# Graph layer on one core: edge sums taken in turned form, without carry products, and crossing runs in one more tile

## Chip, core and metric

One NeuronCore of a Trainium2 chip runs the whole program. The metric is the device time in microseconds. Before the change it is 1387.75 us in the median of three runs (1385.13 to 1388.79).

## What is computed

Per node a row of 256 floats; 50,000 nodes and 12,500 edges. The targets `dst` are drawn unevenly (low numbers more often), the sources `src` evenly.

```python
def L0(x):                       # attention over the edges that end in a node
    h = x @ Wn.T + bn
    e = edge_attr @ We.T + be
    a = leaky_relu(sum((h[src] + e) * attn, -1), 0.01)
    a = exp(a - segment_max(a, dst)[dst])
    a = a / (segment_sum(a, dst)[dst] + 1e-16)
    return relu(segment_sum(h[src] * a[:, None], dst))
def L1(x):                       # mean over the rows of dst, summed by src
    mean = segment_sum(x[dst], src) / maximum(segment_sum(1, src), 1)[:, None]
    return x @ W1.T + b1 + mean @ W2.T + b2
x = layernorm(x + L0(x))
x = layernorm(x + L1(x))
```

## The kernel before, in words

The edges lie in T = 100 tiles of 128, four of them a group (GT = 4), so Q = 25 groups. The nodes lie in G = 98 groups of 512. Five stages follow each other.

1. **Sort.** The edges are ordered by target, then by source, by counting with one-hot products (`sort`, `tiles`, `starts`). `ordered_rows`, `ordered_columns` and `ordered_ends` (L896 to L923) turn the ordered keys into columns and into indices: `idx_src` and `idx_dst` for gathers, `idx_out` for scatters. `idx_out` holds the node in the last edge of a run of equal keys of a tile and a spare row or a number out of bounds elsewhere. For targets this runs inside the second sort; POOL then gathers the 100 tiles of `x[src]` into `X`. For sources it is hung into the node pass by `hooks` at groups HOOK = 48, 50 and 52.
2. **Logits and softmax** on VectorE (L1087 to L1141), with the row ends turned by PE. `weight` is the exponential of each edge, not yet divided.
3. **Target pass** (`by_dst`). `select` (L1024) makes per tile a matrix `sel` that is the edge's weight where row and column have the same key, and `csel` that marks which edges continue the run of the tile before. `aggregate` (L1324) takes `sel` times the tile's rows of `X`, plus `csel` times the summed rows of the tile before; so each tile waits for the ACT copy (`raw`, L681) of the one ahead of it. Column 256 of `X` is one, and its sum is the denominator. `scale` (L1045) divides, `turn_sums` (L1340) turns the rows by PE, ACT copies them to `xT`, `products` (L1279) multiplies by `wnT` on top of a bias product, ACT cuts at zero into `xin`, and POOL adds the rows into `z_dram` (L532), a copy of x. SP waits for all these adds before it loads the first nodes.
4. **Node pass** (`dense`). SP loads 512 nodes, VectorE takes statistics and normalises, PE turns (L1276) and multiplies by `w1T` (L1287), ACT scales, SP stores into `out`. Meanwhile POOL orders the sources and gathers `z[dst]` into `X`.
5. **Source pass** (`by_src`). The neighbours' sums are made as in stage 3, with `csel`, 258 columns (standard deviation and mean of each neighbour ride along) and `scale`. POOL gathers each edge's own node from `z_dram` (L484), VectorE normalises it, PE turns it, and `products` adds the terms with `w2T` and `w1T`. VectorE takes statistics, ACT writes `yout`, POOL scatters the rows over `out` (L487). DVE's turn q holds the own rows of group q and the result of group q - 2.

The engines run their lists in order. Around the change POOL's list sets the order:

```python
for q in range(Q + 3):
    ...
    if q >= 3:
        h = q - 3
        pool.wait_ge(s_ey, GT * h + GT)
        if q < Q:
            pool.wait_ge(s_xs[q % 4], 16 * GT * (q // 4 + 1))
        for j in range(GT):
            scatter(out, yout[h % 4][:, j, :], column(idx_out[SRC], GT * h + j), s_ysc[h % 4])
```

## Time and profile before

| | |
|---|---|
| median of 3 runs | 1387.75 us |
| profiled execution, its own time | 1386.75 us |
| its span in the trace | 1384.9 us |
| mean granted TensorE clock | 0.951 |
| PE, DVE, ACT, POOL busy | 86%, 77%, 52%, 54% |
| target pass, first to last scatter-add issued | 382 to 584 us |
| node pass, first load to last product | 588 to 1023 us |
| source pass | 1024 us to the end |

POOL is busy while it makes an indirect DMA; the transfer itself lands later. "issue" in the chain or behind an idle time means that the profile shows nothing that was waited for.

### The profile page before, as it was taken

To read this page: it belongs to the slowest core of one execution; us is meant where nothing else is said; L and a number is where in the kernel's file an instruction comes from. 1 tells how busy PE (TensorE), PEld (TensorE's weight loads), DVE (VectorE), ACT (ScalarE), POOL (GpSimd) and SP (SyncE) were. 2 spreads that over 40 slices of the span, in tenths; PEclk is the share of its full clock that TensorE was granted. 3 is DMA by queue.
4 is the path that set the end of the run, shared out by engine and by line. 5 is a ranking of instruction groups with operands and counts; after the bars stand their busy time and mean duration, and the time that the engine had idled before them with its cause. 6 is when DMAs were issued, how large, how long until landed. Compare 5 with 4: busy or idle time off the path is not lost.

```text
span 1384.9 us, 25745 instructions
## 1 busy us (share of the span) xinstructions
PE 1195.2 (86%) x6722; PEld 1032.0 (75%) x6722; DVE 1072.2 (77%) x4008; ACT 721.6 (52%) x1720; POOL 753.4 (54%) x731
## 2 busy tenths in 40 slices
PE   4778868970499999689999999999989998889994
PEld 3667758860388888478888888888868887778783
DVE  8799978889655555189999999999988876776761
ACT  4755764540144444357777767777754553434441
POOL 1077754777677777734444005565443565555663
PEclk9999999995699999889999999999999999999997
DMA  5999695878166666557777769999951322222221
GB/s 158 318 266 265 166 248 180 264 230 327 43 92 93 100 96 87 65 201 244 243 243 243 251 236 306 324 324 322 327 181 64 100 90 86 83 87 88 90 75 44
DMA packets 118436, 251.04 MB, mean 181 GB/s; under 512 B 23731, under 2 KB 63548, under 8 KB 118360
## 3 DMA queue, kind: packets, MB, share of 16 engines
q1 hardware_dynamic: 75738, 183.99, 41.7%
q0 software_dynamic: 40128, 64.45, 20.4%
q10 hardware_dynamic: 2494, 1.76, 0.4%
q8 instruction: 27, 0.44, 0.1%
q14 instruction: 49, 0.40, 0.1%
HBM read 172.65 MB, written 130.41 MB: 219 GB/s over the span
## 4 chain that ended last, share of the span: by engine, by line
PE 50%; DMA 12%; POOL 11%; DVE 11%; issue 9%; ACT 5%; SPq 1%; POOLq 0%; ACTq 0%; DVEq 0%
PE bank L1287 30%; PE bank L1276 8%; DMA xin<-z_scratch,idx_src 5%; POOL out_rows L487 5%; POOL xin L484 5%; PE bank L1337 4%; PE bank L1333 3%; PE bank L1264 3%; DMA X<-in_x,idx_src 2%; DVE X L769 2%; ACT aggn L624 2%; DVE bank L772 2%; DMA yout<-low_digits_scratch 2%; DVE xT L772 2%; DVE stats L936 2%
## 5 line engine op out<-in xcount | busy, mean ns | idle before, releaser
L1287 PE MATMUL bank<-w1T,xT 128*128 128x256 f32 x1968 | 459.2, 380 | 0.3 <-ACT yout L586 0.3
L1287 PEld LDWEIGHTS bank<-w1T,xT 128*128 128x128 f32 x1968 | 365.5, 190 | 48.4 <-issue 0.9
L493 POOL DMA_INDIRECT order_scratch<-pay,rank_i x200 | 194.7, 973 | 200.1 <-DVE xin L769 89.9
L936 DVE BATCH_NORM_STATS2 stats<-xin 128x6 f32<-128x512 f32 x246 | 158.7, 687 | 88.5 <-DMA xin<-z_scratch,idx_src 67.0
L577 ACT COPY xT<-bank 128x512 f32<-128x512 f32 x346 | 203.3, 589 | 19.8 <-PE bank L1276 11.7
L586 ACT ACTIVATE yout<-bank,rstd 128x256 f32<-128x256 f32 x492 | 207.3, 489 | 5.2 <-DVE rstd L1177 4.8
L685 ACT COPY agg<-bank 128x257 f32<-128x257 f32 (+1 forms) x200 | 74.3, 372 | 225.0 <-PE bank L1337 218.4
L532 POOL DMA_INDIRECT z_scratch<-xin,idx_out x100 | 156.4, 1564 | 53.2 <-ACT xin L698 30.0
L936 DVE BATCH_NORM_STATS2 stats<-bank 128x6 f32<-128x512 f32 x246 | 165.6, 682 | 22.8 <-PE bank L1287 22.7
L487 POOL DMA_INDIRECT out_rows<-yout,idx_out x100 | 100.0, 1000 | 139.3 <-DMA xin<-z_scratch,idx_src 73.5
L581 ACT ACTIVATE std<-stats,eps_c 128x4 f32<-128x4 f32 x271 | 81.0, 300 | 178.8 <-DVE stats L936 176.6
L769 DVE TENSOR_SCALAR xin<-xin,low_mean,rstd 128x256 f32<-128x256 f32 x492 | 170.7, 410 | 1.0
L484 POOL DMA_INDIRECT X<-z_scratch,idx_dst x100 | 96.0, 960 | 126.6 <-DVE xin L769 91.8
L1264 PE MATMUL bank<-sel,agg 128*128 128x196 f32 x800 | 156.8, 340 | 3.5 <-DVE bank L772 3.5
L1276 PE MATMUL bank<-ident,xin 128*128 128x128 f32 x984 | 133.4, 275 | 19.8 <-DVE xin L769 19.7
L1337 PE MATMUL bank<-agg,csel 128*128 128x257 f32 (+1 forms) x396 | 123.7, 394 | 24.9 <-ACT agg L685 24.9
L1276 PEld LDWEIGHTS bank<-ident,xin 128*128 128x128 f32 x984 | 117.9, 143 | 35.8 <-issue 20.2
L1264 PEld LDWEIGHTS bank<-sel,agg 128*128 128x128 f32 x800 | 133.5, 195 | 4.9 <-DVE bank L772 4.5
L1215 PE MATMUL bank<-X 128*128 128x196 bf16 x800 | 95.8, 256 | 36.4 <-ACT sel L672 21.2
L1333 PE MATMUL bank<-X,sel 128*128 (+2 forms) x400 | 122.7, 390 | 3.4 <-DVE csel L769 3.4
L484 POOL DMA_INDIRECT X<-in_x,idx_src x100 | 99.8, 998 | 45.4 <-issue 19.5
L484 POOL DMA_INDIRECT xin<-z_scratch,idx_src x100 | 99.6, 996 | 42.1 <-issue 30.5
(201 smaller groups left out, 1747.9 us busy)
## 6 DMA issues: line engine op xcount, KB each, us to landing
z_scratch<-in_x SPq DMA_DIRECT2D x125, 400.0 KB
xin<-z_scratch SPq DMA_DIRECT2D x97, 512.0 KB, 5.1
out_rows<-yout SPq DMA_DIRECT2D x97, 512.0 KB, 3.3
kB<-sorted_scratch SPq DMA_DIRECT2D x50, 256.0 KB, 3.4
yout<-keys_scratch SPq DMA_DIRECT2D x50, 128.0 KB
xin<-in_edge_attr SPq DMA_DIRECT2D x12, 512.0 KB, 9.9
yout<-low_digits_scratch SPq DMA_DIRECT2D x50, 64.0 KB
order_scratch<-pay,rank_i POOLq DMA_INDIRECT x200
```

What stands on the lines that cost most here:

```text
L484: g.indirect_dma_start(out=dst_ap, out_offset=None, in_=table, in_offset=where).then_inc(s, 16)
L487: g.indirect_dma_start(out=table, out_offset=where, in_=src_ap, in_offset=None, bounds_check=N - 1, oob_is_err=False).then_inc(s, 16)
L493: g.indirect_dma_start(out=order_dram[k], out_offset=bass.IndirectOffsetOnAxis(ap=rank_i[k][:, t:t + 1], axis=0), in_=pay[:, t, :], in_off ...
L577: a.copy(xT[dst_i][:].rearrange("p a b c -> p (a b c)"), src_bank[:, :]).then_inc(copied, 1)
L586: a.activation(yout[hu][0:rows, j, :], bank_of(j // 2)[0:rows, (j % 2) * D:(j % 2 + 1) * D], ACT.Copy, scale=rstd[0:rows, slot, j:j + 1]). ...
L769: return v.tensor_scalar(o, i, s1, s2, o0, o1) if o1 is not None else v.tensor_scalar(o, i, s1, s2, o0)
L936: return v.bn_stats(stats[0:rows, slot, 2 * p:2 * p + 2, :].rearrange("p j s -> p (j s)"), pair.rearrange("p j c -> p c j"))
L1264: ins = mm(bank[3 + t % 4][:, 0:HC], onehotT[n % 2][:, b, j * P:(j + 1) * P], table[i % 2][:, b, :], start=b == 0, stop=b == 1)
L1276: ins = tr(o[:, at:at + n], buf[0:n, 2 * p + jj, c * P:(c + 1) * P], ident[0:n, 0:n])
L1287: ins = mm(to, buf[:, jj, c, 0:n], w[:, c, :], start=not biased and i + c == 0, stop=i == len(terms) - 1 and c == 1)
L1333: ins = mm(o, sel[u % 2][:, j, :], rows, start=True, stop=first)
L1337: ins = mm(o, csel[u % 2][:, j, :], before, start=False, stop=True)
```

## The change

- The sums are made in turned form: `aggregate` takes `X` as the stationary operand and `sel` as the moving one, so that a bank holds 128 channels by four tiles of 128 edges. What `products` needs on its left is then a copy of that bank (`keep_sums`, `turned_sums`). The turning of the sums, their copies into `xT` and the scaling by VectorE go.
- `csel` and the chain from tile to tile go. A run that crosses a border of tiles is left out by `idx_out` (`ordered_ends`), and is made in one more tile after the last group: `keep_columns` saves the sums at the first and last edge of each tile, `crossing_sums` adds them up by scans, and one product of 100 rows and one gather or scatter with `idx_fix` (`crossing_indices`) follow in each pass.
- The sums of weights and the counts of the sources come from scans over the rows of keys (`run_scans`, `carried_sums`, `run_totals`), for targets before the first scaling, for sources in the node pass by new hooks at groups 49, 51, 53 and 55.
- Target pass: the product with `wnT` is divided and gets the bias (`bn_b`) on VectorE (`scale_h`), and ACT cuts at zero in place; the bias products and `biases` go. Source pass: the weight in `sel` is the reciprocal deviation times the reciprocal count (`per_edge`), and the mean is taken out by centring `w2T` over its inputs (`bias_into_weights`). `X` has 256 columns, not 258.
- POOL, source pass: scatters wait for the gathers of the group before and for the scatters of the group before.
- PE's two edge passes are written out in full, and PE's order in them changes.

```diff
+            pool.wait_ge(s_fix, 1)
+            pool.wait_ge(s_relu, 2 * Q + 1)
+            g.indirect_dma_start(out=z_dram, out_offset=bass.IndirectOffsetOnAxis(ap=idx_fix[:, 0:1], axis=0),
+                                 in_=xin[Q % 4][0:T, 0, :], in_offset=None, compute_op=ALU.add).then_inc(s_zsc[Q % 4], 16)
...
+                if q == Q:
+                    gather(xin[(G + q) % 4][0:T, 0, :], z_dram, column(idx_fix, 2), s_xs[q % 4])
...
-                    pool.wait_ge(s_ey, GT * h + GT)
-                    if q < Q:
-                        pool.wait_ge(s_xs[q % 4], 16 * GT * (q // 4 + 1))
+                    pool.wait_ge(s_ey, GT * h + (GT if h < Q else 1))
+                    if q <= Q:
+                        pool.wait_ge(s_xs[(q - 1) % 4], 16 * GT * ((q - 1) // 4 + 1))
+                    if h >= 1:
+                        pool.wait_ge(s_ysc[(h - 1) % 4], 16 * GT * ((h - 1) // 4 + 1))
                     for j in range(GT):
-                        scatter(out, yout[h % 4][:, j, :], column(idx_out[SRC], GT * h + j), s_ysc[h % 4])
+                        if h < Q:
+                            scatter(out, yout[h % 4][:, j, :], column(idx_out[SRC], GT * h + j), s_ysc[h % 4])
+                    if h == Q:
+                        scatter(out, yout[h % 4][0:T, 0, :], column(idx_fix, 1), s_ysc[h % 4])
...
+            def keep_sums(k, q, u, c, b, users):
+                act.wait_ge(s_agg[k], 2 * q + c + 1)
+                for s, n in users:
+                    wait(act, s, n)
+                wait(act, s_cols[k], q - 1)
+                a.copy(agg[u % 2][:, c, :], bank[b][:, :]).then_inc(s_raw[k], 1)
...
+            def run_scans(values):
+                v.tensor_tensor_scan(fwd[:], same[:, 0:P], values, 0.0, ALU.mult, ALU.add)
+                v.tensor_tensor_scan(bwd[:, ::-1], same[:, 1:P + 1][:, ::-1], values[:, ::-1], 0.0,
+                                     ALU.mult, ALU.add).then_inc(s_ends, 1)
...
+            def run_totals(k, values):
+                kr = krow[k]
+                ts(tmp_r[:], kr[:], ccol[:, 2:3], ccol[:, 0:1], ALU.is_equal, ALU.mult)
+                ts(pen[:, 0:P], kr[:], ccol[:, 3:4], ccol[:, 1:2], ALU.is_equal, ALU.mult)
+                then(v.tensor_tensor(fwd[:], fwd[:], bwd[:], ALU.add))
+                v.tensor_tensor(tmp_r[:], tmp_r[:], pen[:, 0:P], ALU.add)
+                then(v.tensor_tensor(fwd[:], fwd[:], values, ALU.subtract))
+                then(v.tensor_tensor(fwd[:], fwd[:], tmp_r[:], ALU.add))
+                if k == DST:
+                    then(ts(fwd[:], fwd[:], TINY, None, ALU.add))
+                v.reciprocal(fwd[:], fwd[:]).then_inc(s_tot, 1)
...
+            def keep_columns(k, q, u):
+                dve.wait_ge(s_raw[k], 2 * q + 2)
+                ends = agg[u % 2][:].rearrange("p c (j s) -> p c j s", j=GT)[:, :, :, ::P - 1]
+                v.tensor_copy(edge_cols[:, :, bass.ds(GT * q, GT), :], ends).then_inc(s_cols[k], 1)
+            def crossing_sums(k):
+                dve.wait_ge(s_cols[k], Q)
+                v.memset(carried[:, :, 0:1], 0.0)
+                then(v.tensor_tensor(goes_on, prevk[k][:, 1:T + 1], prevk[k][:, 0:T], ALU.is_equal))
+                for c in range(2):
+                    ins = v.tensor_tensor_scan(carried[:, c, 1:T + 1], goes_on, edge_cols[:, c, :, 1], 0.0, ALU.mult, ALU.add)
+                then(ins)
+                for c in range(2):
+                    ins = v.tensor_tensor(crossing[:, c, :], edge_cols[:, c, :, 0], carried[:, c, 0:T], ALU.add)
+                ins.then_inc(s_cross[k], 1)
...
-                wait(dve, s_agg[k], GT * (q - 1))
+                wait(dve, s_agg[k], 2 * (q - 1))
                 if k == SRC:
                     slot = 4 + par
                     dve.wait_ge(s_nsq, q + 1)
                     v.reciprocal(rstd[:, slot, :], std[:, slot, :]).then_inc(s_rc[slot], 1)
-                    dve.wait_ge(s_rc[slot], counted(m, u, off, 2) + 1)
-                    tiles4 = X[:, bass.ds(GT * q, GT), :]
-                    v.tensor_copy(tiles4[:, :, D:D + 1].rearrange("p j c -> p (j c)"), std[:, slot, :])
-                    v.tensor_copy(tiles4[:, :, D + 1:XW].rearrange("p j c -> p (j c)"), stats[:, slot, :, 1])
+                    dve.wait_ge(s_rc[slot], 2 * counted(m, u, off, 2) + 1)
+                    v.tensor_tensor(per_edge[:, par, :], rstd[:, slot, :], per_count[:, bass.ds(GT * q, GT)],
+                                    ALU.mult).then_inc(s_rc[slot], 1)
+                    dve.wait_ge(s_rc[slot], 2 * counted(m, u, off, 2) + 2)
                 for j in range(GT):
                     t = q * GT + j
-                    by = weight[:, bass.ds(t, 1)] if k == DST else rstd[:, slot, j:j + 1]
-                    ts(sel[par][:, j, :], kB[par][:, j, :], keyc[k][:, bass.ds(t, 1)], by, ALU.is_equal, ALU.mult)
-                    ins = ts(csel[par][:, j, :], kB[par][:, j, :], prevk[k][:, bass.ds(t, 1)], lastrow[:, 0:1],
-                             ALU.is_equal, ALU.mult)
+                    by = weight[:, bass.ds(t, 1)] if k == DST else per_edge[:, par, j:j + 1]
+                    ins = ts(sel[par][:, j, :], kB[par][:, j, :], keyc[k][:, bass.ds(t, 1)], by, ALU.is_equal, ALU.mult)
                 ins.then_inc(s_sel[k], 1)
-            def scale(k, q, u):
...
+            def src_counts():
+                dve.wait_ge(s_totT, 2)
+                v.tensor_copy(per_count[:], bank[3][:, 0:T])
+            hooks = {HOOK: lambda: ordered_rows(SRC), HOOK + 1: src_scans, HOOK + 2: lambda: ordered_columns(SRC),
+                     HOOK + 3: src_carries, HOOK + 4: lambda: ordered_ends(SRC), HOOK + 5: src_totals,
+                     HOOK + 7: src_counts, G - 3: first_neighbours, G - 1: lambda: select(SRC, 0, 0, 0, 0)}
...
+            run_scans(wrow[:])
             dve.wait_ge(s_wT, 1)
             v.tensor_copy(weight[:], bank[3][:, 0:T]).then_inc(s_wc, 1)
             dve.wait_ge(s_wc, 1)
             select(DST, 0, 0, 0, 0)
+            dve.wait_ge(s_endsT, 2)
+            carried_sums(bank[7][0:1, 0:2 * P].rearrange("p (i c) -> p i c", i=2)[:, :, 0:T])
+            select(DST, 1, 0, 0, 1)
+            dve.wait_ge(s_csT, 2)
+            then(v.tensor_copy(ccol[:, 0:2], bank[7][0:T, 2 * P:2 * P + 2]))
+            run_totals(DST, wrow[:])
+            crossing_indices(DST)
+            dve.wait_ge(s_totT, 1)
+            v.tensor_copy(per_den[:], bank[7][:, 3 * P:3 * P + T]).then_inc(s_rden, 1)
+            dve.wait_ge(s_rden, 1)
...
+            def scale_h(o, psum, by, rows=P):
+                return stt(o, psum, by, bn_b[0:rows], ALU.mult, ALU.add)
...
-                        for c in range(2):
-                            ins = mm(to, buf[:, jj, c, 0:n], w[:, c, :], start=not biased and i + c == 0,
-                                     stop=i == len(terms) - 1 and c == 1)
+                    pieces = [(left, w[:, c, :]) for of, w in terms for c, left in enumerate(of(jj))]
...
+            def turned_sums(buf, p):
+                return lambda jj: [buf[:, c, (2 * p + jj) * P:(2 * p + jj + 1) * P] for c in range(2)]
...
-            def aggregate(k, q, m, u, j):
...
+            def aggregate(k, q, c, b):
                 pe.wait_ge(s_sel[k], q + 1)
-                wait(pe, s_raw[k], t - 1)
-                rows = X[:, bass.ds(t, 1), 0:w].rearrange("p a c -> p (a c)")
-                ins = mm(o, sel[u % 2][:, j, :], rows, start=True, stop=first)
-                if not first:
-                    wait(pe, s_raw[k], t)
-                    before = agg[u % 2][:, j - 1, 0:w] if j else agg[(u - 1) % 2][:, GT - 1, 0:w]
-                    ins = mm(o, csel[u % 2][:, j, :], before, start=False, stop=True)
+                for j in range(GT):
+                    ins = mm(bank[b][:, j * P:(j + 1) * P], X[:, GT * q + j, c * P:(c + 1) * P], sel[q % 2][:, j, :],
+                             start=True, stop=True)
                 ins.then_inc(s_agg[k], 1)
```

PE in the target pass, two groups before (`bias` and `ones` are the bias product, `ident,aggn` the turning):

```order
L1333 MATMUL bank<-X,sel 128x257
L1337 MATMUL bank<-agg,csel 128x257
L1276 MATMUL bank<-ident,aggn 128x128 x4
L1333 MATMUL bank<-X,sel 128x257
L1337 MATMUL bank<-agg,csel 128x257
L1276 MATMUL bank<-ident,aggn 128x128 x4
L1333 MATMUL bank<-X,sel 128x257
L1337 MATMUL bank<-agg,csel 128x257
L1284 MATMUL bank<-bias,ones 128x256
L1287 MATMUL bank<-wnT,xT 128x256 x2
L1284 MATMUL bank<-bias,ones 128x256
L1287 MATMUL bank<-wnT,xT 128x256 x2
```

and in the changed kernel, the last three groups and the crossing tile:

```order
L1465 MATMUL bank<-sel,X 128x128 x8
L1400 MATMUL bank<-wnT,agg 128x256 x8
L1465 MATMUL bank<-sel,X 128x128 x8
L1400 MATMUL bank<-wnT,agg 128x256 x16
L1400 MATMUL bank<-wnT,csel 100x256 x2
```

The chain of `sel` and `csel` by tile, the turning and the bias products are gone; eight products of 128 columns stand in one piece, and the crossing tile is two more products.

POOL in the source pass, the end of its list before:

```order
L484 DMA xin<-z_scratch,idx_src 128x256 [waits own_turned]
L484 DMA xin<-z_scratch,idx_src 128x256 x3
L487 DMA out_rows<-yout,idx_out 50000x256 [waits own_z_rows_gathered0,edge_y_ready]
L487 DMA out_rows<-yout,idx_out 50000x256 x3
L487 DMA out_rows<-yout,idx_out 50000x256 [waits edge_y_ready]
L487 DMA out_rows<-yout,idx_out 50000x256 x3
```

and in the changed kernel:

```order
L488 DMA xin<-z_scratch,idx_src 128x256 [waits own_turned]
L488 DMA xin<-z_scratch,idx_src 128x256 x3
L491 DMA out_rows<-yout,idx_out 50000x256 [waits y_scattered0,own_z_rows_gathered3,edge_y_ready]
L491 DMA out_rows<-yout,idx_out 50000x256 x3
L488 DMA xin<-z_scratch,idx_fix 100x256 [waits own_turned]
L491 DMA out_rows<-yout,idx_out 50000x256 [waits y_scattered1,own_z_rows_gathered0,edge_y_ready]
L491 DMA out_rows<-yout,idx_out 50000x256 x3
L491 DMA out_rows<-yout,idx_out 50000x256 [waits y_scattered2,edge_y_ready]
L491 DMA out_rows<-yout,idx_out 50000x256 x3
L491 DMA out_rows<-yout,idx_out 50000x256 [waits y_scattered3,edge_y_ready]
L491 DMA out_rows<-yout,idx_out 50000x256 x3
L491 DMA out_rows<-yout,idx_fix 50000x256 [waits y_scattered0,edge_y_ready]
```

The scatters behind the last group's gathers (24, semaphore 0) now wait for those of group 23 (semaphore 3); one gather and one scatter for the crossing tile are added, and each scatter group waits for the one before it.

## Rows read from the trace of the kernel before

**Rows 1.** The page, chain that ended last, share of the span by engine

```profile
PE 50%; DMA 12%; POOL 11%; DVE 11%; issue 9%; ACT 5%; SPq 1%; POOLq 0%; ACTq 0%; DVEq 0%
```

**Rows 2.** Stretches by stage: length, busy time (instructions) by engine, clock, DMA share, GB/s

```profile
382.00:584.30 202.30, 193.19 (x1032) 161.56 (x1030) 100.61 (x353) 89.53 (x188) 154.90 (x100) 0.98 0.64 90
588.00:1013.00 425.00, 418.06 (x2314) 372.48 (x2315) 392.88 (x1074) 294.95 (x762) 180.10 (x188) 0.99 0.80 271
1024.00:1056.50 32.50, 27.25 (x126) 22.36 (x127) 29.62 (x104) 13.66 (x36) 0.59 (x1) 0.89 0.21 68
1056.50:1345.00 288.50, 268.92 (x1376) 231.61 (x1375) 207.71 (x663) 125.22 (x316) 168.53 (x168) 0.98 0.29 89
1345.00:1385.00 40.00, 19.18 (x101) 16.18 (x99) 8.71 (x24) 10.31 (x26) 15.83 (x16) 0.81 0.14 47
```

**Rows 3.** Chain of waits: start, us, what; softmax's end, then a target group

```profile
363.39 0.32 ACT wrow L679
...
471.30 0.43 PE bank L1333 x2
471.74 0.43 PE bank L1337 x2
472.17 0.44 PE bank L1276 x4
...
474.78 0.11 PE bank L1284
474.89 0.86 PE bank L1287 x4
```

**Rows 4.** Timeline of POOL, target pass: start, us, line [idle before <-releaser]

```profile
375.25 0.96 POOL L493 DMA_INDIRECT order_scratch<-pay,rank_i  x1 [0.30 <-issue]
382.06 1.63 POOL L532 DMA_INDIRECT z_scratch<-xin,idx_out  x1 [5.86 <-ACT xin L698]
...
578.62 1.56 POOL L532 DMA_INDIRECT z_scratch<-xin,idx_out  x1 [0.30 <-issue]
...
584.22 1.56 POOL L532 DMA_INDIRECT z_scratch<-xin,idx_out  x1 [0.31 <-issue]
```

**Rows 5.** Timeline of DVE, node pass: one instruction of each group's turn

```profile
785.91 0.16 DVE L1022 RECIPROCAL rstd<-std 128x4 f32<-128x4 f32 x1
...
790.24 0.16 DVE L1022 RECIPROCAL rstd<-std 128x4 f32<-128x4 f32 x1
...
843.17 0.16 DVE L1022 RECIPROCAL rstd<-std 128x4 f32<-128x4 f32 x1
...
847.46 0.17 DVE L1022 RECIPROCAL rstd<-std 128x4 f32<-128x4 f32 x1
```

**Rows 6.** Timeline of POOL, source pass, one group's gathers and the next scatter

```profile
1141.71 1.13 POOL L484 DMA_INDIRECT xin<-z_scratch,idx_src  x1 [0.30 <-issue]
...
1145.76 0.97 POOL L484 DMA_INDIRECT xin<-z_scratch,idx_src  x1 [0.30 <-issue]
1150.69 1.01 POOL L487 DMA_INDIRECT out_rows<-yout,idx_out  x1 [3.96 <-DMA xin<-z_scratch,idx_src]
```

**Rows 7.** Groups by line, 1070 to 1345 us: count | busy, mean ns | idle before

```profile
L484 POOL DMA_INDIRECT xin<-z_scratch,idx_src x80 | 80.5, 1007 | 24.4 <-issue 24.4
L487 POOL DMA_INDIRECT out_rows<-yout,idx_out x80 | 80.1, 1002 | 90.8 <-DMA xin<-z_scratch,idx_src 70.8 <-issue 20.0
```

**Rows 8.** Stretch of the softmax's chain on VectorE, columns as in rows 2

```profile
354.30:363.40 9.10, 1.33 (x8) 0.76 (x8) 6.84 (x27) 0.01 (x1) 6.97 (x8) 0.50 0.02 1
```

**Rows 9.** Timelines of DVE and ACT, source pass: own rows' statistics, rows of yout

```profile
1149.83 1.30 DVE L936 BATCH_NORM_STATS2 stats<-xin 128x6 f32<-128x512 f32 x2 [3.91 <-DMA xin<-z_scratch,idx_src]
...
1155.29 1.57 ACT L586 ACTIVATE yout<-bank,rstd 128x256 f32<-128x256 f32 x4 [0.44 <-DVE rstd L1177]
```

**Rows 10.** Stretches with TensorE less than full, in the sort

```profile
160.00:190.00 30.00, 20.61 (x177) 15.23 (x175) 29.97 (x160) 29.16 (x78) 23.03 (x23) 0.94 0.89 234
190.00:220.00 30.00, 21.91 (x127) 19.19 (x128) 17.40 (x89) 8.67 (x16) 5.70 (x6) 0.83 0.65 159
```

More of the change, by code:

```diff
@@ L540, in _ @@
             pool.wait_ge(s_idx, 2)
[L541 removed]
+            pool.wait_ge(s_agg[DST], 2 * Q)
             for t in range(T):
@@ L1306, in _ @@
             pe.wait_ge(s_wcen, 1)
-            for b in range(2):
-                ins = mm(bank[4][:, 0:D], ones[:], w1T[:, b, :], start=b == 0, stop=b == 1)
+            for o, w in ((bank[4], w1T), (bank[5], w2T)):
+                for b in range(2):
+                    ins = mm(o[:, 0:D], ones[:], w[:, b, :], start=b == 0, stop=b == 1)
             ins.then_inc(s_wsum, 1)
```

423 lines of the change are left out of this document (240 added, 183 removed).

## The prediction

> **What bounds the kernel now.** I read the chain of waits first, then the stretches by stage, then the timelines of one group in each edge pass. The chain gives TensorE half of the span and DMA, POOL and VectorE a ninth each [rows 1], so more than one limit is at work. The stretches [rows 2] part them: the target pass runs from 382 to 584 us, the node pass from 588 to about 1013, the source pass from about 1024 to the end.
>
> In the **target pass** TensorE is busy 193 of 202 us. Its chain [rows 3] shows that a recorded f32 product is two passes of the array. A group of four tiles holds eight passes through `sel` (0.43 us a pair, 1.73), eight through `csel` (1.73), eight transposes (0.87), four bias products (0.43) and 16 passes of `wnT` (3.46): 8.2 us, 25 times. POOL's scatter-adds are close behind. Where they wait for nothing they follow each other in 1.87 us, also over a group's border: 578.62 to 584.22 is three of them [rows 4]. Four take 7.47 us.
>
> In the **node pass** TensorE is at 418 of 425 us, and VectorE is hardly behind: its turn, from one reciprocal of L1022 to the next, is 4.33 us, and 4.29 us where it catches up [rows 5]. What VectorE is given there is paid almost whole.
>
> In the **source pass** the counts per group are 1.73 + 1.73 + 1.75 (16 transposes) + 6.9 (32 passes of `w2T` and `w1T`) = 12.1 us of TensorE. But the 21 groups from the first scatter at 1056.5 to the one at 1345 take 288.5 us [rows 2], 13.74 each. POOL sets that: it issues four gathers of a group, stands until they have landed (last gather at 1145.76, next scatter at 1150.69 [rows 6]), then issues four scatters of an older group. By the groups of lines [rows 7] a gather costs (80.5 + 24.4) / 80 = 1.31 us, a scatter (80.1 + 20.0) / 80 = 1.25 and with the gap of a later one about 1.32: eight are 10.5 us, and the wait for landing adds the other 3.2.
>
> **The change, part by part.** The sum goes against the profiled execution (1386.75 us, 1.0 below the median of the runs shown).
>
> *Start of the target pass.* Two more VectorE operations stand ahead of the target indices, for which POOL's gathers wait: +0.5. The dropped bias splitting and the memset of X's extra columns lay beside the ACT one-hots at the start: 0. From the end of the exponential at 363.7 [rows 3] to the first scatter-add at 382.06 [rows 4] the old path is 18.3 us: eight selections, four tiles one behind the other through PE and ACT, scaling, turning, product. The new one adds two scans, the carried sums, run totals, indices of the crossing runs and two rounds through PE; it drops `csel`, the scaling and the turning. I count 36 VectorE operations up to the first scaled h. In the softmax's like chain 27 take 9.1 us less 1.5 of PE waits [rows 8], 0.28 each: 10.1. With the product at half clock (3.5), the two PE rounds (1.3) and ReLU (0.6) that is 15.5, 2.8 less; with the 0.5 it makes **-2**. The same count could be five short or over: -5 to +2.
>
> *The target pass.* TensorE keeps 8 x 2 passes of 128 columns. No 128-column f32 product is in the trace of this stage, but a transpose has that width and its own weight load and takes 0.109 us [rows 3]; so 16 x 0.109 = 1.74, and 3.46 for `wnT`: 5.2 us. VectorE and ACT, now busy 100.6 and 89.5 us for 25 groups [rows 2], 4.0 and 3.6 each, lose more operations than they get. All are under POOL's 7.47, so POOL becomes the bound. From first to last scatter there were 202.2 us; now 101 of them (the crossing tile's is the last) have 100 gaps of 1.867 = 186.7: **-15.5**. The crossing sums and their product hide behind the scatters of groups 22 to 24, since three groups may run ahead; without that cover they would cost about 6. SP loads after the last add has landed, as now.
>
> *The node pass.* VectorE gets the source side's scans, carries, totals and indices: 33 operations x 0.28 = 9.2 us within seven groups; 0.04 a group is given back, and TensorE can wait about 1 us without loss. TensorE's own small transposes, 0.8, lie inside that. **+8** (4 to 11).
>
> *Start of the source pass.* Here VectorE is busy 29.6 of 32.5 us with 104 instructions [rows 2], 0.28 each. A group drops 14 of them (`csel`, two copies into X, scaling) and gets two: 3.4 us, and the first scatter stands behind three groups' turns. That is 10 us at most, less where TensorE's products are last; I take **-7** (4 to 10) for the first scatter, now at 1056.5.
>
> *The source pass.* TensorE has 1.74 + 0.87 + 6.93 = 9.5 us. POOL no longer waits for the gathers just issued but for those of the group before, and for the scatter of the group before, whose rows have landed under four gathers. Two limits are left. POOL's own sum is 10.5, or 11.1 if the 0.88 us that lies between landing and scatter [rows 6] is paid even with the wait met. The other is a loop: gathers of q-1 land 4.07 us after their last issue, their statistics and the y rows of q-3 are done 7.03 us later (1149.83 to 1156.86 [rows 9]), then POOL scatters; with 9.2 us of issues between, two groups take 9.2 + 4.1 + 7.0 + 0.9 = 21.2, one 10.6. I take 10.7. 21 x (13.74 - 10.7) = **-63.8**.
>
> A rule weighs on that price. The gathers of [rows 7] last 1.007 us in the mean, and single ones from 0.97 to 1.13 [rows 6]; VectorE's work will be packed denser under POOL. The Trainium skill (SBUF — State Buffer, "Who interferes with whom") says that a VectorE operation in a two-port mode and GpSimd lock each other out for a whole instruction; by that every issue would be the long kind. From the rows, with 1.13 for a gather and 1.02 for a scatter, a group is 4 x 1.43 + 4 x 1.34 = 11.1: it adds 8 us, and I keep it as an upper bound.
>
> *The end.* In the 40 us from the scatter at 1345 to the end [rows 2] POOL is busy for 16 only and TensorE's last groups decide, now as before. Added are a gather, a product, and POOL's wait for landed scatters, which is bare where no gathers lie between: twice some 3 us if a scatter lands a little sooner than the gathers of [rows 6], less what TensorE saves: **+2.6** (-3 to +8).
>
> Sum: -2 - 15.5 + 8 - 7 - 63.8 + 2.6 = -77.7, so 1309.
>
> **The rivals.** *B, the loop through ACT, not POOL, sets the source pass.* The y rows hang at the end of VectorE's and ACT's turn, and landing may stretch when gathers always share the queue with scatters. With a landing of 7 us instead of 4.07 the loop is (21.2 + 3) / 2 = 12.1 a group: 21 x 1.4 = +29, 1338. For: both limits lie within 0.1 us, so jitter adds. Against: DMA is busy 0.29 of the time there [rows 2], so there is little for a landing to queue behind.
>
> *C, slower: TensorE's clock.* Each group now leaves TensorE idle for 2.3 of 7.5 us in the target pass. The trace grants 0.50 after long idleness and 0.94 and 0.83 where it is busy 69 and 73% [rows 10]; that is between the levels of 2.4 and 1.2 GHz, near the upper. If it stayed at 1.2 GHz in both edge passes, groups would cost 10.4 and 19.1 us: 25 x (10.4 - 8.25) = +54 and 25 x 19.1 - 343 = +134, with +8: about 1583. It decides where the mean clock of the source pass falls under 9.5 / 13.74 = 0.69, and of the target pass under 5.2 / 8.25 = 0.63. Against: at half clock TensorE has no gaps and so would rise again. The Trainium skill (TensorE: Matmul & The Clock Gate, "HAM oscillation") warns of just such bursts between waits that each start cold; the rows just named agree only in part.
>
> *D, the freed wait is worth nothing*, because y of group q-3 still hangs on rows that have only just been gathered and POOL stands at that semaphore instead: source groups stay at 13.7, 1386.75 - 17.5 + 8 - 7 + 2.6 = 1373. Against: VectorE's own wait for those rows begins a whole group earlier in the new order.
>
> **How the numbers follow.** Forecast 0.70, B 0.17, D 0.06, C 0.03, and 0.04 for a time below the bounds of the terms. The forecast's own bounds: all low ends together are improbable, half of them give 1297; the upper ones (11.1 in the source pass, +11, +2) give 1325. To leave out no more than 2 in 10 the range goes on to most of B: 1295 to 1336. Faster by over 0.3% (4 us, about what a measurement of this kernel can tell from no change): 0.96, within: 0.01, slower: 0.03.
>
> **What would show it.** Scatter-adds of L532's kind 1.87 us apart over group borders and the load of the node pass near 570; TensorE busy about 70% there with a granted clock above 0.9; the node pass 8 us longer, lost around its groups 49 to 55 with VectorE as releaser; scatters of out_rows 10.7 us apart by group, with hardly an idle entry released by the gather's DMA. I am wrong if POOL waits for yout by more than 1 us a group (B, D), or if the clock lies under 0.8 (C).

## The result and the profile after

The changed kernel takes **1295.18 us** (median of 4 runs, 1293.71 to 1296.87) against 1386.74 (1385.13 to 1388.79) for the kernel before, a ratio of 0.9339 with a 95% interval of 0.932 to 0.9359. That is 91.6 us less; I had forecast 77.7 less, 1309. The profiled execution spans 1291.9 us (before: 1384.9); it is the fastest of the four, so its stretches sum to 93.0 less. Its stretches, columns as in rows 2, answer to [rows 2]: the start of the target pass, the target pass, the node pass, the start of the source pass, 21 groups of it, the tail.

```profile
361.00:376.90 15.90, 13.07 (x74) 11.52 (x75) 12.03 (x46) 4.69 (x9) 10.01 (x11) 0.79 0.19 52
376.90:565.40 188.50, 133.22 (x738) 116.93 (x736) 66.79 (x210) 53.38 (x95) 157.96 (x101) 0.88 0.72 98
568.00:989.30 421.30, 410.62 (x2264) 363.37 (x2265) 390.24 (x1084) 287.52 (x744) 172.84 (x181) 0.99 0.78 267
989.30:1033.50 44.20, 40.24 (x224) 34.97 (x223) 38.95 (x112) 24.25 (x64) 15.40 (x17) 0.96 0.50 159
1033.50:1254.60 221.10, 210.45 (x1212) 188.42 (x1211) 139.92 (x411) 93.71 (x232) 165.43 (x168) 0.99 0.37 116
1254.60:1291.90 37.30, 17.66 (x86) 14.50 (x84) 10.50 (x30) 9.45 (x24) 17.90 (x18) 0.83 0.17 57
```

With the same marks in both traces (the exponential, first and last scatter-add, first and last load of the node pass on SP, first scatter to out_rows, first scatter of the group h = 21, end of the span) the gain parts like this:

| stretch | before | after | difference | forecast |
|---|---|---|---|---|
| start to the exponential | 363.39 | 361.01 | -2.4 | +0.5 |
| to the first scatter-add | 18.67 | 15.93 | -2.7 | -2.8 |
| to the last scatter-add | 202.16 | 186.82 | -15.3 | -15.5 |
| to the first node load | 3.81 | 4.21 | +0.4 | 0 |
| to the last node load | 414.8 | 421.4 | +6.6 | +8 |
| to the first scatter of out_rows | 53.7 | 44.1 | -9.6 | -7 |
| 21 groups of the source pass | 288.5 | 221.2 | -67.4 | -63.8 |
| tail | 39.8 | 37.3 | -2.5 | +2.6 |

Timeline of POOL in the target pass, first two and last two scatter-adds, and SP's first load of the node pass behind them [rows 4]:

```profile
376.94 1.63 POOL L535 DMA_INDIRECT z_scratch<-xin,idx_out  x1 [2.88 <-ACT xin L713]
378.88 1.60 POOL L535 DMA_INDIRECT z_scratch<-xin,idx_out  x1 [0.30 <-issue]
...
561.90 1.56 POOL L535 DMA_INDIRECT z_scratch<-xin,idx_out  x1 [0.30 <-issue]
563.76 1.62 POOL L540 DMA_INDIRECT z_scratch<-xin,idx_fix  x1 [0.31 <-issue]
```
```profile
567.97 1.76 SPq L434 DMA_DIRECT2D xin<-z_scratch  x4
```

The 100 gaps are 1.868 us in the mean, over group borders too, and TensorE is busy 133 of 188 us. Groups by line in the source pass, 1033.5 to 1251 us, answer to [rows 7]:

```profile
L491 POOL DMA_INDIRECT out_rows<-yout,idx_out x84 | 84.0, 1000 | 51.8 <-issue 48.9 <-ACT yout L603 2.9
L488 POOL DMA_INDIRECT xin<-z_scratch,idx_src x82 | 79.6, 971 | 25.0 <-issue 18.3 <-DMA out_rows<-yout,idx_out 5.8 <-ACT yout L603 0.9
```

The 70.8 us behind the gathers' DMA are gone (of the 48.9 behind "issue" 22.0 lie ahead of the first scatter, outside the groups). A gather with its gap is 1.27 us and a scatter 1.30, so four of each are 10.3 us; the 21 groups average 10.53. A timeline of POOL over the border to the 13th group (h = 12) shows where the other 0.2 comes from:

```profile
1157.63 0.95 POOL L488 DMA_INDIRECT xin<-z_scratch,idx_src  x1 [0.30 <-issue]
1159.54 1.02 POOL L491 DMA_INDIRECT out_rows<-yout,idx_out  x1 [0.96 <-ACT yout L603]
1162.27 1.01 POOL L491 DMA_INDIRECT out_rows<-yout,idx_out  x1 [1.72 <-issue]
```

At eight of the 21 borders POOL stands 0.45 to 1.10 us instead of the usual 0.30, 3.1 us more in all; the longer of these waits end with the y rows: the loop of the prediction, just under POOL's sum. Another 1.4 us is one pause of 1.72 us inside the 13th group, behind "issue"; nothing here shows its cause.

### The profile page after: what moved, and what is told of

It is laid out like the page before. It is cut to its first block and busy times, and to the rows that moved or that the text cites. A ratio compares the mean times of both kernels' runs of the same rounds, so it can differ in the third digit from the quotient of the medians.

```text
span 1291.9 us, 23301 instructions
## 1 busy us (share of the span) xinstructions
PE 1070.2 (83%) x6258; PEld 940.2 (73%) x6258; DVE 968.0 (75%) x3610; ACT 647.4 (50%) x1525; POOL 752.0 (58%) x731
## 5 line engine op out<-in xcount | busy, mean ns | idle before, releaser
L535 POOL DMA_INDIRECT z_scratch<-xin,idx_out x100 | 156.3, 1563 | 33.1 <-issue 28.9
L488 POOL DMA_INDIRECT X<-z_scratch,idx_dst x100 | 95.6, 956 | 129.6 <-DVE xin L788 93.6
L594 ACT COPY xT<-bank 128x512 f32<-128x512 f32 x247 | 145.4, 589 | 11.9 <-PE bank L1391 7.0
L1465 PE MATMUL bank<-sel,X 128*128 128x128 f32 x800 | 108.2, 286 | 21.9 <-ACT agg L702 16.2
L1465 PEld LDWEIGHTS bank<-sel,X 128*128 128x128 f32 x800 | 103.0, 200 | 28.8 <-ACT agg L702 20.3
L488 POOL DMA_INDIRECT xin<-z_scratch,idx_src x100 | 96.8, 968 | 46.2 <-issue 23.5
L791 DVE SCALAR_TENSOR_TENSOR xin<-bank,xdot,bn_b 128x256 f32<-128x256 f32 x100 | 42.2, 478 | 96.6 <-DMA z_scratch<-xin,idx_out 79.4
```

The costliest lines, as they stand in the source:

```text
L488: g.indirect_dma_start(out=dst_ap, out_offset=None, in_=table, in_offset=where).then_inc(s, 16)
L535: g.indirect_dma_start(out=z_dram, out_offset=column(idx_out[DST], GT * q + j), in_=xin[q % 4][:, j, :], in_offset=None, compute_op=ALU.ad ...
L594: a.copy(xT[dst_i][:].rearrange("p a b c -> p (a b c)"), src_bank[:, :]).then_inc(copied, 1)
L1465: ins = mm(bank[b][:, j * P:(j + 1) * P], X[:, GT * q + j, c * P:(c + 1) * P], sel[q % 2][:, j, :], start=True, stop=True)
```

## The experiments

All times are medians of four or five runs; the kernel before ran beside them at 1382.95 to 1386.18 us.

### Which part of the source pass paid: the wait or the shorter work

e1, in the changed kernel:

```diff
-                    if q <= Q:
-                        pool.wait_ge(s_xs[(q - 1) % 4], 16 * GT * ((q - 1) // 4 + 1))
+                    if q <= Q:
+                        pool.wait_ge(s_xs[q % 4], 16 * GT * (q // 4) + 16 * (GT if q < Q else 1))
```

e2, in the kernel before:

```diff
-                    if q < Q:
-                        pool.wait_ge(s_xs[q % 4], 16 * GT * (q // 4 + 1))
+                    if q < Q:
+                        pool.wait_ge(s_xs[(q - 1) % 4], 16 * GT * ((q - 1) // 4 + 1))
+                    if h >= 1:
+                        pool.wait_ge(s_ysc[(h - 1) % 4], 16 * GT * ((h - 1) // 4 + 1))
```

> The changed kernel, but in the source pass POOL again waits until the four gathers it has just issued have landed. My theory (the freed wait is what paid): a group costs POOL's 10.3 to 10.5 us of issues plus the 3.2 to 3.9 us in which it stands, 13.7 to 14.1, as before the change, though TensorE and VectorE keep their shorter work; 21 groups give 66 to 75 us back, so 1361 to 1370 us. Rival (the shorter work of TensorE and VectorE paid, the wait only filled a gap they left): groups stay near 10.5 us, 1295 to 1300 us.

> The kernel before, with nothing changed but POOL's waits in the source pass: it waits for the gathers of the group before and for the scatters of the group before. My theory (two limits, one behind the other): POOL is freed, but TensorE's passes of this kernel, 12.1 us a group, are the next limit; groups go from 13.74 to 12.1 to 12.6 us, 21 x 1.1 to 1.6 = 24 to 34 us less, 1352 to 1363 us. If the wait were the whole matter, groups would come to 10.7 us and the time to about 1323. If the wait was worth nothing by itself, 1387.

e1 took 1345.37 us (ratio 0.9706, 0.9686 to 0.9725), e2 1357.98 (0.9799, 0.9778 to 0.982). The stretch of e2's 21 groups:

```profile
1056.50:1311.30 254.80, 254.80 (x1345) 223.76 (x1344) 206.33 (x662) 123.62 (x314) 164.86 (x168) 1.00 0.33 101
```

TensorE is busy in all of it, 12.13 us a group, the 12.1 counted in the prediction: the freed wait alone gives 33.7 us and then meets TensorE. The rest of the change gives the other 33.6 (254.8 to 221.2). Neither is the cause alone. e1 came out 16 to 25 us faster than I expected: most of its groups take 12.7 to 12.8 us (21 of them 271.2, 12.9 in the mean), not 13.7. So the 13.74 of the kernel before held something that e1 no longer has.

### The missing microsecond: a load that collides

The timelines of POOL and SP, one group of the kernel before:

```profile
1145.76 0.97 POOL L484 DMA_INDIRECT xin<-z_scratch,idx_src  x1 [0.30 <-issue]
1150.69 1.01 POOL L487 DMA_INDIRECT out_rows<-yout,idx_out  x1 [3.96 <-DMA xin<-z_scratch,idx_src]
```
```profile
1145.94 0.32 SPq L410 DMA_DIRECT2D kB<-sorted_scratch  x1
```

and of e1:

```profile
1159.89 0.95 POOL L488 DMA_INDIRECT xin<-z_scratch,idx_src  x1 [0.30 <-issue]
1163.57 1.02 POOL L491 DMA_INDIRECT out_rows<-yout,idx_out  x1 [2.73 <-issue]
```
```profile
1157.13 0.32 SPq L417 DMA_DIRECT2D kB<-sorted_scratch  x1
```

In the kernel before SP issues the load of kB (256 KB, started by VectorE's last selection) 0.18 us behind the last gather, and POOL stands 4.93 us from there to its scatter. In e1 VectorE is done sooner, the load lies 2.76 us ahead, and it is 3.68. The 21 groups of before sort themselves: 13 (the expectation below counts 14) with the load -0.1 to +0.4 us from the last gather have 4.5 to 5.1 us, six with it at +2.8 or later or with none left have 3.6 to 3.7, and two between (at -1.0 and +2.1) have 4.2 and 4.7. (The one with 4.7 says nothing of the load: the same group, h = 4, has 4.85 in e1 and 4.66 in e7, wherever the load lies.) Only SP is changed in e7:

```diff
             for q in range(2, Q):
+                if q >= 3:
+                    sp.wait_ge(s_xs[(q - 3) % 4], 16 * GT * ((q - 3) // 4 + 1))
                 load3(SRC, q)
```

> The kernel before with one wait added on SP: in the source pass the load of the broadcast keys kB (256 KB) starts only when the gathers of its group have landed. In the kernel before this load is issued 0.16 to 0.4 us behind the last gather in 14 of 21 groups, and there POOL stands 4.5 to 5.1 us from the issue of the last gather to the first scatter; in the six groups where it comes over 2.5 us later, or no load is left, it is 3.6 to 3.7 us. My theory (the two transfers share the DMA engines and the landing is late by that): all groups come to 3.65 us, 12.75 us a group instead of 13.74, 21 us less, 1364 to 1368 us. Rival (the landing is late for another reason, as VectorE's denser work or TensorE's): no change, 1386 us, or slower if VectorE now waits for kB.

It took 1371.01 us (0.9904, 0.9888 to 0.992), 3 to 7 above what I expected. With the load at +2.7 us or later, or none left, the gap is back to 3.6 to 3.8 in 20 of 21 groups; POOL, then SP:

```profile
1155.60 0.97 POOL L486 DMA_INDIRECT xin<-z_scratch,idx_src  x1 [0.31 <-issue]
1159.28 1.01 POOL L489 DMA_INDIRECT out_rows<-yout,idx_out  x1 [2.71 <-DMA xin<-z_scratch,idx_src]
```
```profile
1158.41 0.32 SPq L410 DMA_DIRECT2D kB<-sorted_scratch  x1
```

One wait more on the queue made the old kernel 13 us faster. The groups came to 13.0 us in the mean, not 12.75: from the first scatter to the last gather they take 9.27 us, as in the kernel before (9.28), and 9.13 in e1; why was not tried. e7 also tells what e1's gain is. From the last gather to the scatter the 21 groups stand 93.6 us in the kernel before, 79.4 in e1 and 78.2 in e7. So 14.2 of the 17.4 us that e1's groups gain are this stretch, and e7 gets all of it with the old, longer work on TensorE and VectorE: as long as POOL waits for the landing, the shorter work pays by moving the load and by little else. The Trainium skill (DMA: Bandwidth & Descriptors, "Queues, rings and completion order") says that each DMA engine goes round between the queues that have work, a packet at a time; by that a gather waits its turn behind packets of the load, and these rows agree in direction, with 0.8 to 1.5 us for 256 KB.

In the changed kernel all loads but one still fall within 1.3 us of the last gather. POOL has stopped waiting for that landing, but VectorE still does, and the y rows hang on VectorE. Its first statistics of landed rows start 2.8 to 4.7 us behind the last gather; in the last three of the 21 groups, where no load is left, 2.7 to 2.8. One group with the load and one without, POOL's last gather, SP's load, VectorE's statistics:

```profile
1147.33 0.94 POOL L488 DMA_INDIRECT xin<-z_scratch,idx_src  x1 [0.30 <-issue]
1147.67 0.32 SPq L417 DMA_DIRECT2D kB<-sorted_scratch  x1
1151.55 1.30 DVE L1024 BATCH_NORM_STATS2 stats<-xin 128x6 f32<-128x512 f32 x2 [3.83 <-DMA xin<-z_scratch,idx_src]
```
```profile
1232.77 0.95 POOL L488 DMA_INDIRECT xin<-z_scratch,idx_src  x1 [0.30 <-issue]
1235.49 1.30 DVE L1024 BATCH_NORM_STATS2 stats<-xin 128x6 f32<-128x512 f32 x2 [2.51 <-DMA xin<-z_scratch,idx_src]
```

All eight borders at which POOL stands longer than 0.30 us follow a group whose rows came 3.96 us or later (here 4.22, and 7.99 us behind the statistics the scatter at 1159.54); two more such groups are followed by no stand, and no earlier landing is followed by one. So the load seems to cost the changed kernel up to these 3.1 us by way of the y rows. e7's wait was not tried in the changed kernel, so this is read from its trace and not shown by a run.

### What bounds a source group now

e4 adds to VectorE, behind the statistics of the landed rows:

```diff
+                    for r in range(4):
+                        if n_own == P:
+                            v.bn_stats(more_stats[:, r, :], own[:, 2 * (r % 2):2 * (r % 2) + 2, :].rearrange("p j c -> p c j"))
```

e5 adds to POOL, ahead of the scatters:

```diff
+                    g.memset(spare[:], 0.0).then_inc(s_spare, 1)
+                    pool.wait_ge(s_spare, h + 1)
```

e3 takes from POOL:

```diff
-                    if q <= Q:
-                        pool.wait_ge(s_xs[(q - 1) % 4], 16 * GT * ((q - 1) // 4 + 1))
-                    if h >= 1:
-                        pool.wait_ge(s_ysc[(h - 1) % 4], 16 * GT * ((h - 1) // 4 + 1))
```

e8 is e3 with VectorE's two blocks for the products moved ahead of its wait for landed rows (and on ACT the root and the y rows ahead of the root of the landed rows, alike):

```diff
+                if in_range(q, 2, Q + 3):
+                    dve.wait_ge(s_er, 2 * (q - 2) + len(sets(n_edge)))
...
+                    dve.wait_ge(s_esq, q - 1)
+                    v.reciprocal(rstd[0:n_edge, 2 + u % 2, :], std[0:n_edge, 2 + u % 2, :]).then_inc(s_erc, 1)
                 if isinstance(q, int) and q == Q:
                     crossing_sums(SRC)
                 if in_range(q, 0, Q + 1):
                     dve.wait_ge(s_xs[u], 16 * GT * m + 16 * (GT if n_own == P else 1))
```

> The changed kernel with four more statistics operations of VectorE per group of the source pass, between the statistics of the landed rows and those of the products: 4 x 0.6 = 2.4 us. VectorE would be busy 9.3 of 10.5 us, so it is no bound by its own sum. If POOL's issues alone bound the pass: 0 to +4 us. If the loop (gathers land, VectorE and ACT make the y rows three groups older, POOL scatters them) lies just under POOL's sum, as in my prediction: two groups cost 2.4 us more, less what slack there is, so +0.8 to +1.2 us a group, +17 to +26 us, 1312 to 1321 us.

> The changed kernel with one more POOL instruction per group of the source pass, a memset of 128x512 f32 whose end POOL waits for, ahead of the scatters. Such a memset takes 0.57 us at the start of the kernel; with the usual gap it is 0.6 to 0.9 us. If POOL's own issues bound the groups: the whole of it in each of 22 groups, +13 to +20 us, 1308 to 1315 us. If the loop over two groups binds instead, POOL's addition counts once in two groups: +7 to +10 us, 1302 to 1305 us. If TensorE (9.5 us) or VectorE bound it, nothing.

> The changed kernel without both of POOL's waits in the source pass (for gathers of the group before, and for scatters of the group before). In the steady groups both are met when POOL comes to them, so these stay at 10.5 us. In the tail, where no gathers lie between, POOL stands 2.0, 2.3, 2.2 and 4.35 us for landed scatters; without that the scatters hang on the y rows (the last y row is written 10.9 us before the last scatter starts) and the last group's scatters, some 5.2 us: about 6 us less, 1287 to 1291 us. Rival (y rows decide the tail as in the kernel before, and the wait for the group before costs in the steady groups too): less than 2 us in the tail, and steady groups shorter by the same at each.

> The changed kernel without POOL's two waits in the source pass, and with VectorE and ACT making the y rows of the group two back before they wait for the newly landed rows, so that the loop is cut: y rows no more hang on gathers just issued. If the loop lies just under POOL's sum and costs the excess of a few groups (in the changed kernel 21 groups take 221.2 us, 4.5 more than 21 x 10.3), the steady groups all come to 10.3 us, 4 us less than the kernel without waits (1288.0 us); the first scatter comes 1 to 2 us sooner too: 1281 to 1284 us. Rival (the excess is POOL's own jitter, or landed scatters): 1286 to 1289 us. It could be slower if VectorE's turn now stands idle for TensorE's products and TensorE gets its rows later.

| kernel | time, us | ratio (95%) | 21 groups | tail |
|---|---|---|---|---|
| changed | 1295.18 | 0.9339 (0.932 to 0.9359) | 221.2 | 37.3 |
| e4 | 1323.28 | 0.9549 (0.9527 to 0.9571) | 241.9 | 39.5 |
| e5 | 1317.21 | 0.9518 (0.9501 to 0.9536) | 241.5 | 38.6 |
| e3 | 1288.01 | 0.9293 (0.9276 to 0.931) | 221.1 | 31.5 |
| e8 | 1281.06 | 0.9248 (0.9236 to 0.9261) | 216.3 | 28.2 |

e4's groups go 10.27 and 12.7 in turn, +1.0 in the mean for 2.4 us of VectorE: the loop over two groups, as expected, and 0.2 of slack. Another 5.3 us lie ahead of the first scatter and 2.2 in the tail; with these, which I had not counted, e4 came out above the 1312 to 1321 expected. e5's groups go from 10.53 to 11.5; the memset and the wait for it are 1.1 us by the trace:

```profile
1169.44 0.54 POOL L579 MEMSET spare<- 128x512 f32 x1
1170.94 1.03 POOL L493 DMA_INDIRECT out_rows<-yout,idx_out  x1 [0.95 <-POOL spare L579]
```

so all of it is paid but the part for which POOL had stood for y rows (I had the price of the memset too low). Both limits of the prediction are there, 0.2 us apart. e8 parts them: with the loop cut no border stands longer than 0.30 us and all groups take 10.27 to 10.44, 4.9 us less in 21. Only 3.1 of these are the borders'. 1.4 are the pause in the 13th group: it is there, 1.4 to 2.0 us with the usual gap, in every kernel of this document but e8, e10 and e11, and why it is not in those isn't shown. e3 leaves the steady groups at 10.53, so POOL's two waits are met there, and takes 5.8 us off the tail, where they are bare. From the timeline of POOL, changed kernel, then e8:

```profile
1266.77 0.98 POOL L491 DMA_INDIRECT out_rows<-yout,idx_out  x1 [0.30 <-issue]
1270.03 0.98 POOL L491 DMA_INDIRECT out_rows<-yout,idx_out  x1 [2.28 <-DMA out_rows<-yout,idx_out]
```
```profile
1182.40 0.98 POOL L491 DMA_INDIRECT out_rows<-yout,idx_out  x1 [0.30 <-issue]
1183.69 0.98 POOL L491 DMA_INDIRECT out_rows<-yout,idx_out  x1 [0.30 <-issue]
1184.98 0.99 POOL L488 DMA_INDIRECT xin<-z_scratch,idx_src  x1 [0.30 <-issue]
```

That the first scatter would come 1 to 2 us sooner in e8 was wrong: from the exponential it is 673.3 us, in the changed kernel 672.5. e8's time lies in the range expected because of 3.3 us that I had not named, in the tail: e3 still stands 1.91 and 2.08 us there for y rows, e8 doesn't.

### The node pass: what VectorE's additions cost

e6 leaves out the source side's scans, carried sums and run totals; a memset of one column stands for each:

```diff
-                same_keys(SRC)
-                run_scans(ones[0:T, :])
+                v.memset(same[:, 0:1], 0.0).then_inc(s_ends, 1)
...
```

> The changed kernel without the source side's scans, carried sums and run totals in the node pass (the counts per node are then left out of the result; a memset of one column stands for each step). In the trace these operations hold VectorE from 792.23 to 793.20, 801.54 to 804.38 and 813.39 to 816.12 us, 6.5 us in all, less 0.3 for the memsets. If VectorE's time in the node pass is paid whole: 5.5 to 6.3 us less, 1289 to 1290 us. Rival (TensorE, busy 410 of 421 us there, was the bound and the node pass grew for another reason, as later gathers or slower products): under 2 us.

1290.7 us (0.9317, 0.9303 to 0.9331): the interval still touches the changed kernel's, so the size is read from the trace. One VectorE instruction of each turn, changed kernel:

```profile
792.13 0.16 DVE L1106 RECIPROCAL rstd<-std 128x4 f32<-128x4 f32 x1
797.02 0.16 DVE L1106 RECIPROCAL rstd<-std 128x4 f32<-128x4 f32 x1
801.46 0.15 DVE L1106 RECIPROCAL rstd<-std 128x4 f32<-128x4 f32 x1
808.20 0.15 DVE L1106 RECIPROCAL rstd<-std 128x4 f32<-128x4 f32 x1
813.31 0.16 DVE L1106 RECIPROCAL rstd<-std 128x4 f32<-128x4 f32 x1
821.00 0.16 DVE L1106 RECIPROCAL rstd<-std 128x4 f32<-128x4 f32 x1
```

and e6:

```profile
794.10 0.16 DVE L1106 RECIPROCAL rstd<-std 128x4 f32<-128x4 f32 x1
...
818.51 0.17 DVE L1106 RECIPROCAL rstd<-std 128x4 f32<-128x4 f32 x1
```

Five turns take 28.9 us (4.89, 4.44, 6.74, 5.11, 7.69), 24.4 in e6 and 22.7 in the kernel before. The additions cost 6.2 us, nearly the node pass's +6.6; the 6.5 us of work left out in e6 gave 4.5 back. By turn: the scans, 1.0 us of VectorE, cost 0.4; the carries, 2.8, cost 1.7; the totals, 2.7, cost 2.6. So up to 1.1 us of a turn's addition is absorbed, but in the totals' turn only 0.1.

### The target pass: is there room on TensorE

```diff
                     for p in range(2):
                         wait(pe, s_hb, 2 * (h - 2) + p + 1)
+                        if p == 0:
+                            products(rbank(h % 2, p), [(turned_sums(agg[h % 2], p), wnT)])
```

> The changed kernel with the products of wnT for the first pair of tiles made twice in every group of the target pass: TensorE's work goes from 5.2 to 5.2 + 1.73 = 6.9 us a group, under POOL's four scatter-adds of 1.867 us, 7.47. If POOL alone bounds the pass: the 100 gaps stay at 1.867 us, the first scatter-add comes some 0.9 to 1.8 us later, 1296 to 1298 us. If TensorE's clock or the chain from sums to h had no room left (the granted clock of the pass is 0.88 in the mean): up to 25 x 1.73 = 43 us more. A clock nearer 1.0 is expected, since TensorE idles less.

1295.78 us (0.9355, 0.9327 to 0.9384): no change. The scatter-adds stay 1.87 us apart; the first comes 17.65 us behind the exponential, 1.7 later. The same stretch, changed kernel, then e9:

```profile
460.00:490.00 30.00, 22.87 (x126) 19.89 (x125) 11.09 (x36) 8.92 (x16) 25.12 (x17) 0.94 0.74 103
```
```profile
460.00:490.00 30.00, 30.00 (x173) 27.30 (x172) 12.53 (x40) 10.17 (x19) 25.12 (x17) 1.00 0.74 108
```

The changed kernel's idle TensorE costs it some granted clock (0.94), and that costs nothing, since POOL bounds the pass.

### A faster version

e10 is e8 with five moves, of which these are the shortest to show: on VectorE in the target pass, on POOL, and on VectorE in the source pass.

```diff
-                if in_range(q, 1, Q - 1):
+                if in_range(q, 1, Q - 1) and not first:
                     select(DST, q + 1, m, u, 1)
...
+                        if first and p == 0:
+                            select(DST, q + 1, m, u, 1)
+                    if first:
+                        keep_columns(DST, h, u - 1)
+                        crossing_indices(DST)
...
-                pool.wait_ge(s_relu, 2 * q + 2)
+                pool.wait_ge(s_relu, 2 * q + (2 if q else 1))
...
+                    if q == 0 and j == 2:
+                        pool.wait_ge(s_relu, 2)
...
+                if isinstance(q, int) and q == 3:
+                    crossing_indices(SRC)
```

On TensorE the carries are turned between the two halves of the first sums, and the first product comes ahead of the second sums. e11 is e10 with one number changed on POOL, and the source side's run totals in two turns of VectorE (with the copy of the counts moved later, to group G - 5):

```diff
-            order_src(20)
+            order_src(16)
```

> The kernel with the y rows first (1281.1 us) and, besides, a shorter way to the first scatter-add of the target pass and less VectorE work in the node pass: the carries are turned between the two halves of TensorE's first sums instead of behind them, the first group's product is made ahead of the second group's sums, the selection of the third group and the indices of the crossing runs come behind the first group's scaling, POOL starts the first group after its first two tiles; the source side's indices of crossing runs are made in the source pass, where VectorE has room. From the exponential to the first scatter-add it is 15.9 us in the changed kernel; I expect 11 to 12.5, since VectorE loses a wait of 1.8, 1.0 of indices and 1.2 of selection from the way, and POOL starts 1.6 earlier, less what TensorE then lacks. The turn of the node pass with the totals, 7.69 us, goes to 6.6. Together 4 to 6 us less, 1275 to 1277 us. Rival (TensorE at half clock there, or the POOL queue, sets the start): under 1.5 us, 1280 us.

> The kernel of all changes together (1275.6 us), with 16 instead of 20 of the source side's order scatters ahead of the target pass on POOL (the other four come in the node pass, where POOL is idle), and the source side's run totals made in two turns of VectorE in the node pass instead of one. In the kernel before it POOL's last order scatter starts at 373.37 and the first scatter-add at 374.63 us, 0.31 us behind it: POOL's own queue had become what holds it. Without four scatters POOL is free 5.1 us sooner and the h rows decide, 1 to 2.5 us sooner. Of the turn with the totals, 6.7 us, the experiments let me expect 0.5 to 1 us back when it is two. Together 1.5 to 3 us less, 1272.5 to 1274 us. Rival (the h rows come just as late): under 1 us.

e10 took **1275.63 us** (0.9212, 0.9187 to 0.9238), by the ratios 1.4% less than the changed kernel. The turn with the totals fell from 7.69 to 6.57 us. The way to the first scatter-add fell from 15.9 to 13.7, not to the 11 to 12.5 expected, so part of the gain lies elsewhere and was not followed up. At that start POOL's own queue of order scatters had become the limit (columns as before; e10's timeline of POOL):

```profile
373.37 0.96 POOL L497 DMA_INDIRECT order_scratch<-pay,rank_i  x1 [0.30 <-issue]
374.63 1.64 POOL L537 DMA_INDIRECT z_scratch<-xin,idx_out  x1 [0.31 <-issue]
```

e11 removed that and won nothing: 1275.12 (0.9223, 0.9208 to 0.9238), the rival of its expectation. In its profiled execution POOL stands 5.84 us for the h rows and the first scatter-add comes 14.1 us behind the exponential, because the first product ran at the lower clock. The same eight passes, e10, then e11, from the timelines of PE:

```profile
368.44 1.99 PE L1412 MATMUL bank<-wnT,agg 128*128 128x256 f32 x8 [0.68 <-ACT agg L700]
```
```profile
367.00 3.78 PE L1424 MATMUL bank<-wnT,agg 128*128 128x256 f32 x8 [0.68 <-ACT agg L700]
```

The granted clock from the exponential to the first scatter-add was 0.75 in e10 and 0.57 in e11, near the level of 1.2 GHz; TensorE did the same before in both. The split turns took 5.25 and 5.55 us instead of 6.57 and 4.34: nothing either.

## Why the prediction was right, and where it was off

The verdict, the order of the terms and the size of most were right. That the time lies inside my range is luck: 1295.18 is 0.2 us above its low end of 1295, two of the four runs lie under it, and to a time below the bounds I had given only 0.04. Each miss was small, but most have one sign: the tail 5.1 us, the source pass 3.6, the way to the exponential 2.9 (mostly chance), the start of the source pass 2.6, the node pass 1.4. By its own steps:

- *Start of the target pass, -2.* From exponential to first scatter-add it was -2.7 against -2.8. The two operations more in the indices (+0.5) don't show: everything ahead of the exponential was 2.4 us shorter in this execution. Little of that is the change's: in the ten profiles of the changed kernel and of those built on it the exponential begins between 359.5 and 363.9 us (mean 361.5), in the three of the old kernel and its variants at 361.3, 362.0 and 363.4.
- *Target pass, -15.5.* -15.3. POOL's 1.867 us is the bound, TensorE's 5.2 us a group was nearly right (133 us for 25, 5.3 each), and e9 shows 1.7 us more is covered. One sign was missed: the granted clock of the pass is 0.88, where I had written above 0.9; it cost nothing here.
- *Node pass, +8.* +6.6. The sum of the added work, 9.2 us, is 8.2 by the trace (1.0, 2.8, 2.7, 1.1 for the indices, 0.6 for the two more in the ends), and 2 us of it are absorbed, where I had allowed 1. The flat 0.28 us hid an error the other way: one of the operations, the reciprocal of 100x128, takes 0.95 us. The Trainium skill (VectorE: DVE Perf Modes, "First, the fixed hardware budget") says reciprocal is an iterated divide; beside 0.28 us for an addition of the same shape the rows agree.
- *Start of the source pass, -7.* -9.6, near the upper end of what I gave. That VectorE was the limit there more than TensorE is suggested by e4, whose additions on VectorE cost 5.3 us ahead of the first scatter.
- *Source pass, -63.8.* -67.4. The step that was off is the term for POOL's sum: 10.5 us from the mean of gathers and gaps in [rows 7], 10.3 measured. My means held the long gathers of the kernel before (1007 ns; now 971). The step on the loop, 21.2 us for two groups, is what the trace shows where it binds: 1138.27 to 1159.54 is 21.3. It binds only behind a late landing; e4 and e8 show it just beside POOL. That I read the landing in the kernel before as one price, 4.07 us, missed that it is 2.8 where no load lies near, and that the rest was the kB load.
- *Tail, +2.6.* -2.5, the largest miss, and the one step whose path was wrong. The bare waits came as foreseen (2.0, 2.3 and 2.2 us, and the last scatter behind landed ones), but I had put TensorE's last groups, 12.1 us each then, as deciding: with 9.5 they are done early, and the last y row is ready 10.9 us before its scatter.

Of the rivals, *B* had the loop right and its price wrong: landing took 2.7 to 4.7 us and not 7, and groups 10.5 and not 12.1. *C* fell: the clock was 0.88 and 0.99 in the two passes. *D* fell, by e1 against the changed kernel: 50 us for the wait. Of the two-port lock of the Trainium skill (SBUF — State Buffer, "Who interferes with whom"), by which I kept 11.1 us as an upper bound, this trace shows no such price: gathers became shorter, 971 ns.

## What to carry to other kernels

Count each engine's work per group before freeing a wait: here the wait alone was worth 34 us, and the shorter work alone 17, nearly all of that by moving a load; together they were worth 67, because TensorE's 12.1 us a group stood right behind the wait. When a queue stands for a landing, look at what another queue issued within a microsecond of it; in this kernel one wait that moved a load was worth 13 us. When a queue has become the bound, let no other engine's program order tie its operands to the transfers it has just issued; here that tie cost 3 us in the groups and 3 in the tail.

## Not expected of the hardware

- A 256 KB load issued -0.1 to +0.4 us from an indirect gather delays that gather's landing by 0.8 to 1.5 us (13 groups of the kernel before); issued 2.6 us or more before or behind it, the time from the last gather to the scatter is 3.6 to 3.8 us, but for h = 4 in both e1 and e7 and one group of 3.97 in e1.
- TensorE took 1.99 or 3.78 us for the same eight passes after 20 us at a granted clock of 0.50 and the same work since, in two kernels whose TensorE work does not differ up to there (e10, e11, one profiled execution each). A forecast of the time to a first result after such a stretch should leave room for that.
- With TensorE busy 76% in a stretch of the target pass the granted clock was 0.94, and 1.00 when it was full (e9).
